# Four layers of attention and feed-forward: new planner costs for the causal attentions, and the third one's sums written back into PSUM

## The reference

```python
q = (x @ Wq).reshape(B, T, H, Dh)
k = (x @ Wk).reshape(B, T, H, Dh)
v = (x @ Wv).reshape(B, T, H, Dh)
scores = jnp.einsum('bthd,bshd->bhts', q, k)
mask = jnp.tril(jnp.ones((T, T), dtype=scores.dtype))
scores = scores * mask
attn = jax.nn.softmax(scores / T ** 0.5, axis=-1)
out = jnp.einsum('bhts,bshd->bthd', attn, v).reshape(B, T, H * Dh)
return out @ Wo
```

## Time and profile before

| | us |
|---|---|
| median of 3 runs | 1052.92 (1050.35 to 1055.82) |
| the profiled execution | 1051.1 |
| its span, first to last instruction | 1049.4 |
| mean granted TensorE clock, share of full | 0.984 |

### The profile page before, as it was taken

One profiled execution on the slowest core, in us unless ns is written; L12 is line 12 of the kernel. 1 busy time (PEld: TensorE's weight loads), 2 busy tenths in 40 slices (PEclk: granted clock), 3 DMA queues, 4 the chain that ended last, 5 costly groups with the idle time before them and its releaser, 6 DMA issues. The chain is left out here.

```text
span 1049.4 us, 16975 instructions
## 1 busy us (share of the span) xinstructions
PE 971.5 (93%) x6103; PEld 548.1 (52%) x6103; DVE 697.7 (66%) x1987; ACT 531.3 (51%) x1140; POOL 334.8 (32%) x465
## 2 busy tenths in 40 slices
PE   9999999989999989999999999999999988889896
PEld 3544454676454554433487544455556444445585
DVE  2677774687797994453323467777772788877587
ACT  4566665434888871121101567665544545655442
POOL 4211112233588861000001221112210346662452
PEclk9999999999999999999999999999999979999999
DMA  6000000100001200210000020000000000000001
GB/s 255 2 1 1 2 2 1 56 1 2 8 20 56 85 2 1 103 48 0 1 1 1 1 99 22 2 1 2 1 1 1 2 0 2 1 2 1 2 1 41
DMA packets 4823, 21.64 MB, mean 21 GB/s; under 512 B 489, under 2 KB 1769, under 8 KB 3844
## 3 DMA queue, kind: packets, MB, share of 16 engines
q1 hardware_dynamic: 4740, 20.55, 5.2%
HBM read 19.01 MB, written 1.05 MB: 19 GB/s over the span
## 5 line engine op out<-in xcount | busy, mean ns | idle before, releaser
L995 ACT ACTIVATE PB<-pair 128x1024 f32<-128x1024 f32 (+3 forms) x288 | 223.2, 811 | 137.2 <-PE pair L1780 135.9
L1255 DVE CUSTOM_DVE_ANT_0 junk<-bank,cst 128x128 bf16<-128x128 f32 (+3 forms) x384 | 171.1, 487 | 106.1 <-PE bank L1764 103.9
L826 POOL TENSOR_SCALAR_AFFINE_SELECT PB<-PB 128x256 f32<-128x256 f32 x192 | 78.8, 413 | 309.0 <-ACT PB L995 307.5
L1258 DVE TENSOR_REDUCE pmx<-bank 128x1 f32<-128x512 f32 x192 | 122.5, 684 | 40.6 <-PE bank L1764 39.8
L1764 PE MATMUL bank<-KO_r,QO_r 64*128 64x512 f32 (+3 forms) x576 | 139.9, 412 | 9.5 <-DVE A L1333 5.2
L1798 PE MATMUL pvb<-PB,V 128*32 128x512 f32 (+3 forms) x1152 | 123.2, 499 | 10.5 <-ACT PB L995 8.4
L1764 PEld LDWEIGHTS bank<-KO_r,QO_r 64*128 64x128 f32 x576 | 72.3, 187 | 105.4 <-DVE pmx L1255 40.6
L1776 PE MATMUL pair<-QO_r,KO_r 64*128 64x512 f32 (+3 forms) x576 | 115.2, 391 | 12.6 <-ACT PB L995 10.8
L832 POOL TENSOR_TENSOR parts_r<-y_f,parts_r 128x512 fp32r<-128x512 f32 x24 | 30.8, 1284 | 279.1 <-ACT parts_r L966 279.1
L1780 PE MATMUL pair<-ms,sel_r 64*128 64x512 f32 (+3 forms) x576 | 101.4, 345 | 0.0
L1066 ACT ACTIVATE KO<-pair,nm 128x128 f32<-128x128 f32 x256 | 90.1, 392 | 9.7 <-DVE nm L1478 9.3
(11 more groups left out here) (237 smaller groups left out, 1696.2 us busy)
## 6 DMA issues: line engine op xcount, KB each, us to landing
WF<-in_moe_gu SPq DMA_DIRECT2D x1, 3520.0 KB, 12.4
WF<-in_tern_w SPq DMA_DIRECT2D x1, 3072.0 KB, 10.2
WA<-in_w_att SPq DMA_DIRECT2D x2, 1024.0 KB, 10.4
V<-in_moe_d SPq DMA_DIRECT2D x1, 1792.0 KB, 7.3
xT<-in_xT SPq DMA_DIRECT2D x2, 512.0 KB, 5.8
WA<-in_w_att SPq DMA_DIRECT2D x2, 512.0 KB, 7.2
X<-in_x SPq DMA_DIRECT2D x1, 1024.0 KB, 10.8
A<-in_rope SPq DMA_DIRECT2D x1, 1024.0 KB, 4.8
```

The costliest lines, as they stand in the source:

```text
L826: pool.affine_select(p2, p2, pattern=[[0, 2], [1, P]], compare_op=ALU.is_ge, fill=0.0, base=0, channel_multiplier=-1).then_inc(causal, 1)
L995: act.activation(pb[:, st % 2, 2 * i:2 * i + 2, 0:n], ps[:, :, 0:n], ACT.Exp, scale=scale)\
L1255: r_done(dve.tensor_tensor_reduce(junk[:, (r_used - 1) % 3, 0:n], ps[:, 0:n], tri[:, HALF - n:HALF], 1.0, LOWEST, ALU.add, ALU.max, accum_ ...
L1258: r_done(dve.tensor_reduce(to, ps[:, 0:n], AX.X, ALU.max))
```

## The change

Two things, in one diff. First, costs in `attention_plan` (ns): a maximum from 85 to 150 fixed, and to 235 where it is masked; an exponential from 110 to 170 fixed; ScalarE's copies from 540 or 560 to 600, from 1050 to 1150 (`b`) and from 970 to 1025 (`s`); accT of the first two attentions from 620 to 700, that of the last stays at 1300; a norm from 4200 to 3700. The plans of sublayers 0, 4 and 6 are computed anew from them, so the order of items may differ. Second, in the last attention the sum of line 1332 is written in place into the bank in PSUM instead of into `num`, and line 1333 reads it from there. Line 1331 stays as it is.

```diff
         if kind == "max":
             clock.tensor(start, columns(item) * 0.445 + 10)
             for _ in range(TWO):
-                clock.vector(85 + 1.05 * columns(item))
+                clock.vector((235 if item[2] // TH == item[3] else 150) + 1.05 * columns(item))
...
         elif kind == "mT":
             clock.tensor(start, clock.TURN)
-            done[item] = clock.scalar(540)
+            done[item] = clock.scalar(600)
         elif kind == "exp":
             n = columns(item)
             clock.tensor(start, 2 * n * 0.445 + 20)
-            done[item] = clock.scalar(110 + 2 * n * 0.833)
+            done[item] = clock.scalar(170 + 2 * n * 0.833)
...
-                clock.act = max(clock.act, clock.pe + clock.SEEN) + 540
+                clock.act = max(clock.act, clock.pe + clock.SEEN) + 600
...
-            done[item] = clock.vector(620 if s != LAST_ATT else 1300)
+            done[item] = clock.vector(700 if s != LAST_ATT else 1300)
...
         elif kind in ("outT", "new", "x1", "bin_new"):
-                done[item] = clock.scalar(560)
+                done[item] = clock.scalar(600)
...
-                clock.dve += 4200
+                clock.dve += 3700
...
         elif kind == "b":
-            clock.scalar(1050)
+            clock.scalar(1150)
...
         elif kind == "s":
-            done[item] = clock.scalar(970)
+            done[item] = clock.scalar(1025)
         elif kind == "v":
-            done[item] = clock.scalar(560)
+            done[item] = clock.scalar(600)
...
                             step(dve.tensor_tensor(num, w, e.unsqueeze(3).to_broadcast([P, TH, HG, HD]), ALU.mult))
-                            step(dve.tensor_tensor(num, ps[:, :, :, 0:HD], num, ALU.add))
-                            r_done(dve.tensor_tensor(o, num, wide, ALU.mult))
+                            step(dve.tensor_tensor(ps[:, :, :, 0:HD], ps[:, :, :, 0:HD], num, ALU.add))
+                            r_done(dve.tensor_tensor(o, ps[:, :, :, 0:HD], wide, ALU.mult))
```

## The result

The changed kernel takes 1063.68 us (median of 6 runs, 1061.96 to 1066.71), against 1055.39 us for the kernel before (6 runs). The ratio is 1.0093, with a 95% interval of 1.0066 to 1.0119: slower by 0.9%, where I forecast 1049.9 us and put 1040 to 1059 around it. The profiled execution took 1066.4 us, its span 1064.7.

The account below looks back on a forecast made before the run. No engine was full; stages were loops of latencies set by TensorE's queue order, with VectorE limiting the last attention. Profiled 1051.1 - 3.0 + 0 = 1048.1, plus 1.8 for the median: 1049.9 us, range 1040 to 1059.

Parts of the forecast that it names:

- Change 1: Last attention, lines 1332 and 1333: keeping the sum in PSUM frees VectorE from GpSimd's hold, saving 2.99 us.
- the three held operations: Line 1333 at 839.88, 876.67 and 926.49, taking 1.43, 1.47 and 1.49 us beside GpSimd's TENSOR_TENSOR instead of 0.42.
- the second clock fall: Last attention, 880 to 900: 3.2 us at 1.2 GHz; if it goes, 1.6 us gained, left out of the sum.
- The first fall: Last attention, 840 to 860: 12.4 us at 1.2 GHz, begun before 840 and expected to stay.
- The price of writing PSUM: VectorE's line 1332 writing PSUM: taken as 0, within 0.05 us each, or 0.4 us over eight.
- Rival 3: Last attention, line 1331: the hold moves there, up to 1.26 us each, so change 1 gives nothing: 1053 us; chance 0.10.
- Change 2: Planner costs reorder items in all three causal attentions: taken as 0 us, between -6 and +12 over 12 long stages.
- the upper bound of 12: Order drift's worst case: +1 us in each of 12 stages with both query halves, +12 us.
- the steady pattern: Inside stages, the order pv, max, exp, exp, max should mostly stand; changes come at the ends of stages.
- Rival 1: Stage ends: last maxima without exp beside them, ScalarE waits; four stages at 2.4 us, 9.6 us, 1059.5 or 1062; chance 0.18.

Follow-up runs that it names:

- the old plans: Item orders of the kernel before; with lines 1332 and 1333 keeping the sum in PSUM against that kernel: 1049.17 us, ratio 0.9943.
- the costs alone: New planner costs with the sums still in SBUF, against the kernel before: 1067.97 us, ratio 1.012.
- the changed kernel with zeros: Changed kernel plus zero multiplications in TensorE's gaps after accT of the last attention's first two stages: 1059.58 us, ratio 1.0066 to the kernel before.
- the items moved: Sums in PSUM, new plan in the last attention alone, 16 items reordered at its third stage's end: 1058.19 us, ratio 1.0048 to the kernel before.

## Why the prediction was wrong

**Change 1 was right, and larger.** The sum was 2.99 us; measured were 6 us (3.6 to 8.3) on the old plans and 2.8 us on the new, where the intervals overlap. In the traces of the old plans the `ms` copies around the three held operations lie 0.95, 2.09 and 1.02 us closer together, where I had 1.01, 1.05 and 0.93; the excess is in the second place, where the clock fall was. Line 1333 took 424 ns eight times, TensorE's wait on it in the list above fell from 5.2 to 2.3 us, and the second clock fall went, for which I had put 1.6 us into the range only. With it the sum is 4.6, inside the interval (the two profiled executions are 4.0 us apart). The first fall stayed, as I said, but shorter: 840 to 860 has 0.74 for 0.69, and 838 to 840 now 1.00.

**The price of writing PSUM** was taken as 0, within 0.05 us. It is 8 ns (432 against 424), 0.06 us over eight. The Trainium skill ("VectorE: DVE Perf Modes", The TRN2 errata) has a fixed cost of 120 cycles from PSUM against 58 from SBUF. Here 128x256 fp32 with one of its inputs in PSUM took 424 ns and with both in SBUF 424 ns: the measurement decides, for this form of operation.

**Rival 3 didn't happen.** Line 1331 took 424 to 500 ns. What the Trainium skill says ("SBUF — State Buffer", SBUF: two separate sides) holds for GpSimd's TENSOR_TENSOR: 1.47 us beside one, and no hold without it. For TENSOR_SCALAR the traces show less than the whole duration: line 1331 took 0.42 us inside one of 2.00 us, and line 1333 in the kernel with the costs alone took 0.70 us at 998.89, 0.26 us after one of 2.03 us had begun.

**Change 2: here the prediction failed.** The step was "Between these I take 0 since the drift helps where ScalarE waits for scores and hurts where a stage's maxima end last". Measured by ratios the term is +15.8 us with the sums in their bank, beyond even the upper bound of 12, and +12.6 with the sums in SBUF. Two things were wrong in it. The middle between bounds was no estimate but a lack of one. I argued on the steady pattern, which did stand (23.94 us for 24.0 in the first attention, 23.98 for 24.1 in the last), and left the ends of stages to a guess. Rival 1, which had them right in kind, was priced at 9.6 us and given 0.18. And the planner could have been asked: replaying both lists on its clock needs no run and gives +10.9 to +18.7 us. I named its rule, "which engine runs dry first", without noting that a rule that looks one step ahead promises nothing for the sum.

**Rival 1 was right in kind, and explains the last attention better than the first two.** "The last maxima of a stage are left with no exp beside them. ScalarE then waits for m and mT": so it is at 907.90 to 913.93. ScalarE's waits on line 1303 in the last attention add up to 18.5 us, and to 10.0 with the old plans and the same bank edit. But it wasn't four stages at 2.4 us. In the new lists of the first and second attention, too, one score item for maxima stands behind the last exponential in the stretches of (1,1) and (2,1), where the old lists have none, and these keep their length: copies 3 to 4 and 4 to 5 are 23.9 to 24.0 us apart, 23.9 to 24.1 with the old plans. Where the profiled 19.3 us between the old plans and the new (both with the bank edit) lie:

| | measured, us | plan clock, us |
|---|---|---|
| start of the first attention, to its first `ms` copy | +5.1 | |
| first attention, copies 1 to 8 | +3.4 | |
| sublayers 1 to 3 | -1.0 | |
| all up to the first copy of the second attention | +7.5 | +4.4 |
| second attention, and up to the first copy of the third | +2.6 | +5.5 |
| third attention, copies 1 to 8, and the end | +9.2 | +4.9 |

In the last attention copies 3 to 4, with the wait, have +5.0 and copies 1 to 2 have +3.7. In the first attention copies 1 to 2 are 1.9 us closer, copies 2 to 3 are 3.5 and copies 7 to 8 are 2.7 further apart, so stages exchange time, and only the sum tells. No single wait that I found stands for the 3.4 and 4.4 us by which the first and second attention grew, and why they did stays open beyond the costs that made the order. The start moved by 5.1 us in the profiled run, but by 1.8 to 3.4 in two other kernels with the same plan there. The granted clock goes with it. Windows from the span's start to the first copy, for the costs alone, the changed kernel with zeros, and the changed kernel:

```profile
0.00:31.24 31.24, 28.35 (x106) 13.04 (x106) 10.28 (x39) 14.22 (x21) 13.94 (x14) 1.00 0.57 214
```
```profile
0.00:32.84 32.84, 30.70 (x106) 13.70 (x106) 10.28 (x39) 14.20 (x20) 13.97 (x14) 0.95 0.55 204
```
```profile
0.00:34.53 34.53, 30.92 (x106) 14.26 (x106) 10.38 (x39) 14.19 (x20) 13.91 (x14) 0.90 0.52 194
```

The same work has 0, 3.4 and 6.8 us at 1.2 GHz there. The old plans without a fall take 29.43, so 1.8 of the 5.1 us are order and 3.3 go with the clock. Rival 1's price, 2.4 us a stage "less what VectorE idled", left out that accT can stand among the late maxima (2.7 us of VectorE here), and that the clock may fall near such a wait (0.59 in 910 to 920), though with the items moved and a wait of 2.40 us it fell as well.

**The clock.** I wrote that the prediction would be wrong if the clock fell in stages where it held, or if first and third attention moved by over 3 us each. Both came: from first to last copy the first attention took 148.2 us for 144.8, the third 152.1 for 146.5. The mean granted clock over the span is 0.973 after and 0.984 before.

**The chances.** They don't fit each other at rival 1: half of it was said to lie within 1059 us, and most of it (0.17 of 0.18) above 1058.2.

## What to carry to other kernels

Where a program orders work by a model, replay the old order and the new one on that model, with either cost table, before anything else. A planner that looks one step ahead may make a worse list from better durations, above all where it charges an overlapping operation its full duration (VectorE's maxima here, 23 us by that edit alone). Look for the cost of a new order first at the ends of stages, by which engine has nothing else left beside the last items, but add up all stages before you believe it: moving the worst end gained 3.9 us there and gave 2.2 back in the next. A VectorE operation with SBUF inputs only, beside a busy GpSimd, is worth rewriting so that one input comes from PSUM, where the data is there anyway.

## What the hardware showed

The granted clock rose where TensorE's gaps were filled with zeros (30.7 us at 1.2 GHz in the last attention, then none), and a kernel's time goes with its mean clock from run to run. The ten runs of the kernel with moved items go from 1053.47 us at a mean clock of 0.980 to 1064.59 at 0.965. Over 116 runs of 13 kernels, each against its own kernel's mean, 0.01 of mean clock goes with 6.6 us; 0.01 is some 21 us at 1.2 instead of 2.4 GHz, so 0.3 us per us. Zeros that removed 30.7 us of it in one attention gave back only 5.6, so 0.18; at the start of the kernel, where TensorE is busy for nearly the whole stretch (28.35 of 31.24 us), it is 3.3 us for 6.8, so 0.48. What a fall costs here depends on where it falls. That the rest of the correlation is the other way round, longer waits making lower clocks, is a guess.

The hold of VectorE by GpSimd's TENSOR_TENSOR ended 0.3 us after that operation in the cases shown (983.60 + 1.47 against 983.52 + 1.26), and a step of 16 elements was held as well (1.21 us for 0.19). One input in PSUM was enough to be free of it. With the old plans and the bank edit, line 1333 again runs beside a TENSOR_TENSOR in three of its eight executions, and none is over 424 ns (GpSimd and VectorE):

```profile
839.64 1.27 POOL L843 TENSOR_TENSOR WF_r<-WF,cst 128x512 fp32r<-128x512 f32 x1
839.77 0.42 DVE L1333 TENSOR_TENSOR A<-bank,rc 128x256 f32<-128x256 f32 x1
```

Line 1303, which keeps both inputs in SBUF, is still held there (1.21 us the longest of 24).
